# Two edits to the attention half of a fused block: a rewritten order around a pair's values, and half of the band bars as a minimum on VectorE

## What is computed

```
S  = einsum('bcqd,bckd->bcqk', Qc, Kwin)          # 64 queries against 128 keys of two windows
As = [S[band]]                                     # only 64 of the 128 keys count: key > query, key <= query + 64
for l in 1..4: As.append(q . pooled keys of the window before)     # 8 pooled keys a level
mn = min over levels of max(A)
exps = [exp(A - mn) for A in As]
esum = exps[0].sum() + sum(scale_l * exps[l].sum())
out = (exps[0] @ Vwin + sum(scale_l * exps[l] @ Vpooled_l)) / esum
```

## Time and profile before

| | |
|---|---|
| time, median of 3 runs | 287.54 us (284.66 to 290.64) |
| the profiled execution's own time | 287.94 us |
| its span in the profile | 286.1 us |
| mean granted clock of TensorE | 0.964 |
| TensorE matmul busy | 268.0 us, 94% |
| VectorE busy | 161.8 us, 57% |
| ScalarE busy | 149.5 us, 52% |
| GpSimd busy | 134.7 us, 47% |

### The profile page before, as it was taken

How to read it: one execution, slowest core, us unless ns; L and a number is a source line. 1 busy time by engine, 2 the same in 40 slices (tenths; PEclk the granted TensorE clock), 3 DMA queues, 4 the chain that set the end, 5 groups by cost and what they waited for, 6 DMA issues and landing times.

```text
span 286.1 us, 7311 instructions
## 1 busy us (share of the span) xinstructions
PE 268.0 (94%) x2713; PEld 222.8 (78%) x2713; DVE 161.8 (57%) x463; ACT 149.5 (52%) x308; POOL 134.7 (47%) x231
## 2 busy tenths in 40 slices
PE   7999996989997999689989999999999999999994
PEld 6768774878886898659979896778888678888883
DVE  7782460643345402422792266878786987777763
ACT  6764633543474452713738356544686555555551
POOL 7751300230122146204161304886884778888881
PEclk9998898697999999959999999999999999999999
DMA  7211157304009666369675110000000000000000
GB/s 221 61 56 62 57 113 242 73 13 129 2 19 336 231 173 184 94 161 290 135 176 142 39 23 21 2 10 10 11 10 9 10 11 10 9 11 19 9 10 21
DMA packets 19107, 23.04 MB, mean 81 GB/s; under 512 B 8248, under 2 KB 14136, under 8 KB 19072
## 3 DMA queue, kind: packets, MB, share of 16 engines
q1 hardware_dynamic: 17952, 21.69, 26.9%
q10 hardware_dynamic: 1120, 0.89, 1.1%
HBM read 10.93 MB, written 5.24 MB: 57 GB/s over the span
## 4 chain that ended last, share of the span: by engine, by line
PE 69%; DVE 10%; DMA 9%; issue 4%; ACT 3%; SPq 2%; POOL 0%; ACTq 0%; DVEq 0%
PE bank L1138 11%; PE bank L1140 10%; PE bank L1139 10%; PE bank L1330 8%; PE bank L1306 4%; PE bank L1309 4%; DMA k_rows<-arena 3%; PE bank L1292 3%; PE bank L1219 2%; PE bank L1274 2%; PE bank L1181 2%; PE bank L1334 2%; DMA xres<-x 2%; DVE work L1121 2%; PE bank L1232 2%
## 5 line engine op out<-in xcount | busy, mean ns | idle before, releaser
L744 POOL TENSOR_TENSOR work<-work 128x256 f32<-128x256 f32 x110 | 81.7, 747 | 31.5 <-DVE work L1121 18.9
L1121 DVE SCALAR_TENSOR_TENSOR work<-bank,comb,work 128x256 f32<-128x256 f32 x128 | 59.0, 481 | 25.4 <-ACT work L885 23.7
L885 ACT ACTIVATE work<-bank 128x256 f32<-128x256 f32 x128 | 48.5, 385 | 45.6 <-PE bank L1140 41.9
L860 ACT ACTIVATE work<-bank 128x512 f32<-128x512 f32 x64 | 34.8, 594 | 44.1 <-PE bank L1309 32.9
L1330 PE MATMUL bank<-work,vaug 128*64 128x64 f32 x1024 | 42.3, 231 | 0.0
L1330 PEld LDWEIGHTS bank<-work,vaug 128*64 128x64 f32 x1024 | 36.9, 143 | 4.4 <-ACT work L860 0.4
L650 POOL COPY vaug<-vwin 128x64 f32<-128x64 f32 x64 | 12.2, 236 | 53.1 <-PE bank L1334 53.0
L1306 PE MATMUL bank<-bar,ident_r 128*128 128x512 f32 x64 | 31.9, 499 | 1.1 <-issue 0.9
L1309 PEld LDWEIGHTS bank<-qmk,kst 98*128 98x128 f32 x128 | 26.0, 203 | 5.0 <-issue 1.8
L1309 PE MATMUL bank<-qmk,kst 98*128 98x256 f32 x128 | 26.8, 292 | 0.0
L1139 PE MATMUL bank<-arena,xT_hi 128*128 128x512 f32 x64 | 25.1, 392 | 0.0
(11 more groups left out here) (220 smaller groups left out, 541.9 us busy)
## 6 DMA issues: line engine op xcount, KB each, us to landing
w_stage<-w SPq DMA_DIRECT2D x8, 512.0 KB, 4.4
qmk<-qst SPq DMA_DIRECT2D x20, 96.0 KB
qst<-arena SPq DMA_DIRECT2D x12, 128.0 KB, 3.9
kst<-arena SPq DMA_DIRECT2D x9, 128.0 KB, 3.2
qst<-q_rows SPq DMA_DIRECT2D x3, 384.0 KB, 3.9
qmk<-q_rows SPq DMA_DIRECT2D x12, 96.0 KB
p_rows<-kpool SPq DMA_DIRECT2D x2, 512.0 KB, 3.8
attT<-denom SPq DMA_DIRECT2D x8, 128.0 KB, 2.6
```

What stands on the lines that cost most here:

```text
L744: gp.tensor_tensor(gacc[t % 2][:, :], gacc[t % 2][:, :], gtmp[(adds - 1) % TMP_RING][:, :], ALU.add).then_inc(acc_done, 1)
L860: act.activation(prob[lo % P_RING][:, :, :, :], bank[sc % SCORE_BANKS][:, :].rearrange("p (c j q) -> p c j q", c=2, j=GH), ACT.Exp).then_i ...
L885: act.activation(sig[hn % SIG_RING][:, :], bank[hn % HID_BANKS][:, HID:2 * HID], ACT.Sigmoid).then_inc(sig_done, 1)
L1121: dve.scalar_tensor_tensor(dst[:, :], bank[hn % HID_BANKS][:, 0:HID], comb[:, t, e:e + 1], sig[hn % SIG_RING][:, :], ALU.mult, ALU.mult).t ...
```

## The change

Two edits. BARRED_BY_PE shrinks from all eight tiles of a unit to (0, 1, 4, 5): the tiles k = 2, 3, 6, 7 lose the matmul of L1306 and get the minimum of L1060 on VectorE. In the order, ("norm", u) and ("values", u, h) no longer wait in a list for the next out with k % 4 == 1: norm follows directly behind the outs of its step and values at the end of that step. Guards and shift of the next unit, and its transposition and load one step later, stand ahead of the `beside` work of their step and no longer within it. For u = 1 and u = 3 the guards begin at score 4 instead of 3 and 2. ("pl", 1) and ("kp", 1) move from the end of unit 1 and the start of unit 2 to steps 2 and 4 of unit 2.

```
-GUARD_AT = [4, 3, 2, 2, 2, 2, 2]
+GUARD_AT = [4, 4, 2, 4, 2, 2, 2]
...
         s.append(("out", u, k))
-        if k % 4 == 1:
-            s.extend(norms)
-            norms.clear()
         if k % 4 == 3:
             norms.append(("values", u, k // 4))
...
-            7: [("apply", 1, 1)], 8: [("xT", 1, 0)], 9: [("pl", 1)]},
-        2: {0: [("xT", 1, 1)], 1: [("kp", 1)], 3: [("qk", 1, 0, 0)], 4: [("qk", 1, 0, 1)], 5: [("kd", 4)], 6: [("qk", 1, 1, 0)],
+            7: [("apply", 1, 1)], 8: [("xT", 1, 0)]},
+        2: {0: [("xT", 1, 1)], 2: [("pl", 1)], 3: [("qk", 1, 0, 0)], 4: [("qk", 1, 0, 1), ("kp", 1)], 5: [("kd", 4)], 6: [("qk", 1, 1, 0)],
...
             while len(local) > LAG:
                 attend()
+            s.extend(n for n in norms if n[0] == "norm")
+            if u + 1 < UNITS and i == GUARD_AT[u] + 2:
+                s += [("shiftT", u + 1), ("shift load", u + 1)]
+            if u + 1 < UNITS and i == GUARD_AT[u]:
+                s += [("guard", u + 1, 0), ("guard", u + 1, 1), ("shift", u + 1)]
             for n in (i, i + 1):
                 s += beside.get(u, {}).get(n, [])
-                if u + 1 < UNITS:
-                    first = GUARD_AT[u]
-                    if first <= n < first + 2:
-                        s.append(("guard", u + 1, n - first))
-                    if n == first + 1:
-                        s.append(("shift", u + 1))
-                    if n == first + 2:
-                        s.append(("shiftT", u + 1))
-                    if n == first + 3:
-                        s.append(("shift load", u + 1))
+            s.extend(n for n in norms if n[0] == "values")
+            norms.clear()
...
-BARRED_BY_PE = tuple(range(NB // 2))
+BARRED_BY_PE = (0, 1, 4, 5)
```

## The result

| | before | after |
|---|---|---|
| median of 20 runs each, us | 288.27 (284.66 to 293.38) | 280.85 (274.48 to 288.92) |
| ratio, 95% interval | | 0.961 [0.956, 0.967] |
| profiled execution: time, span | 287.94, 286.1 | 277.70, 275.9 |
| mean granted clock of TensorE | 0.964 | 0.975 |

The kernel became 7.4 us faster by the medians (279 was forecast from a before of 288), and 10.2 us by the two profiled executions. Medians here are over all runs; the ratios leave disturbed runs out. All lines of after stand six lower than in the kernel before: the bar L1306 is L1300, the minimum L1060 is L1054, the first score tiles L1292 are L1286, an out's matmuls L1330 are L1324, guards L1219 are L1213.

A forecast was written before the change was run, and what follows sets the result against it. TensorE sets the attention's pace, through matmuls, few long waits and stretches at 1.2 GHz. Stretch gains sum to 14.3 us; less 3.4 for one slow stretch and 2 for unfollowed VectorE waits leaves 8.9, so 279 us, range 271 to 287.

The forecast's parts named there:

- Up to the first score of unit 1: Start to 46.24 us: shift transposed ahead of kp, its load issued earlier; gain 3.0 us, 0.9 of it bars, bounds 2 to 3.5.
- To the pair 4, 5 of unit 1: Up to 54.86 us: the slow 6.83 us takes half at 2.4 GHz if the wait nearly goes; gain 3.4 us, else 0.
- To the first score of unit 2: 54.86 to 66.40 us: VectorE's work delays out 3 and the shift load; 10.6 us for 11.54, gain 0.9.
- To the guards of unit 5, and to the spread: Units 2 and 3 to 109.13 us: gain 1.8 us; unit 4 to 121.53, norm earlier: gain 2.6, bounds 1 to 3.6.
- To the guards of unit 6: Up to 129.8 us: unit 5's keys and queries 4 us sooner, slow stretch gone; gain 3.4 us, else 0.
- Units 5 to 7: Bars -2.8 us against VectorE's queue in unit 6 +2.5, ScalarE +0.5, last minima +0.6: loss 0.8, against 0 to +4.
- Bars that go: 32 matmuls of L1306 at 0.23 us each come off TensorE: 7.4 us, 0.93 a unit, counted inside the stretches.
- TensorE slower at large: Rival: fewer dense matmuls and short waits lower the clock in all units, 3.4 us a unit; 292 to 299 us; chance 0.07.
- VectorE in the way: Rival: minima delay the shift or an out in most units, none of the slow stretches gone; 286 us; chance 0.27.
- All slow stretches go: Rival: every stretch at 1.2 GHz goes, the 68.04 one too; gain 16 us, so 272; chance 0.20.
- The edit doesn't act: Rival: weight loads the bars cover come to light, a third of 0.23 us lost each, 2.5 us; inside the forecast.
- Minima that come: 32 minima on VectorE at 0.71 us each, 22.7 us in all, hidden as a sum; about 1.9 each beside GpSimd.

The follow-up runs named there:

- e1: The kernel before with only half of the bars (tiles 2, 3, 6, 7 on minima), old order kept: 293.8 us, ratio 1.014.
- e13: e2 with guards, shift, transposition and load put back inside the beside work, with the old guard starts: 279.2 us, ratio 0.974.
- e2: The changed kernel with all bars on TensorE as before and no minimum, so the new order alone: 279.3 us, ratio 0.968.
- e8: The changed kernel with unit 1's second statistics and the normalisation behind them moved to score 6, behind the shift's load: 279.1 us, ratio 0.970.
- e10: e2 with norm put back behind the next out with k % 4 == 1: 285.0 us, ratio 0.992.
- e9: e8 plus two SyncE moves: unit 2's output gather ahead of w1's loads, unit 5's keys and head queries ahead of unit 3's gather: 274.8 us, ratio 0.954.
- e4: The changed kernel with neither bars nor minima for tiles 2, 3, 6 and 7: 281.1 us, ratio 0.975.
- e11: e2 with the same three moves as e9, all bars on TensorE and no minimum: 275.9 us, ratio 0.956.
- e3: The changed kernel with its 32 minima and all 64 bars issued on TensorE as well: 281.0 us, ratio 0.970.
- e5: The changed kernel with no bar at all and 64 minima on VectorE: 289.0 us, ratio 0.998.
- e14: e5 with all 64 bars issued on TensorE besides: 287.7 us, ratio 0.989.

## Why the prediction was right in the time and wrong in some of its reasons

**Up to the first score of unit 1.** Right in the mechanism: 3.8 us in the profiled execution (46.24 to 42.44) for 3.0. Some of it is chance: the prediction counted three stretches at 1.2 GHz in the attention, and the fourth, at 27.08 to 30.50, lies in front of this score. e1 and e13, which keep the old place of the load and don't have that stretch, start it at 40.98 and 41.11, wait 2.7 us or more, and reach the score at 44.99 and 45.23. So the move is worth 2.6 to 2.8 us. The 0.9 for bars in the 3.0 was nothing: e2, with all of them, reaches it at 42.41.

**To the pair 4, 5 of unit 1.** Half right: the slow stretch shrank from 6.8 to 3.4 us, gain 2.0 for 3.4. The reserve in the sum, that one of two slow stretches stays, was in the right size: 3.4 us of each stayed.

**To the first score of unit 2.** Right in place and price: 10.69 for the 10.6 forecast, with VectorE's operations ahead of the load, and a wait of 1.1 before an out and 1.1 before unit 2. e8 shows that these two waits hang on the statistics and the normalisation.

**To the guards of unit 5, and to the spread.** 1.9 for 1.8, then 1.65 for 2.6. The second was short because norm was not free to run: its ScalarE copies stood ready but waited 1.75 us for the gather of unit 2 (4.43 us, issued behind SyncE's w1 loads), a queue that I had not followed. In e10, with norm back, TensorE waits 2.2 us at the spread again. In the same stretch I took two VectorE operations of the earlier trace rows for 0.65 us each when alone; L459 takes 0.48 at the median of its eight, and one of them had grown to 2.60.

**To the guards of unit 6.** Wrong by 2.5: 0.9 for 3.4. The slow stretch halved, but the pooled keys of unit 6, which queue behind those of unit 5 that I had coming 4 us sooner, came 2.3 us too late for TensorE. e9 mends that, and with the other two moves gives 6 us.

**Units 5 to 7.** 1.0 of loss for the 0.8 forecast, right by luck in part: half of the new slow stretch at 146.86, 1.7 us, is in it, which the step didn't have. No part of it was tested by itself.

**Bars that go. This is the step that failed.** I counted 32 x 0.23 = 7.4 us of it in the sum, 0.93 in each unit. The duration was right; that it comes off the time was not. By e2 and e4 half of it (3.6) reaches the rest; 2.1 us show up as more idle time in the profiled executions, and where the remainder goes isn't shown. The minima take back 2.1 (e4 to after), with idle up by another 2.5; that leaves 1.5. And 6.6 us more at 1.2 GHz in after than in e2 would take 3.0; these two means have errors of 1.8 and 1.9 us and come from different groups, and e9 and e11 don't repeat the difference, so this last part is not shown for after. What is shown is the outcome: in the new order, three pairs that differ in the second edit or its bars alone (e2 and after, e3 and after, e11 and e9) are within 1% of each other. So the second edit is worth nothing within 1%, and the first edit made the gain. That the total came out right is in part luck: the profiled execution of after had 13.7 us at 1.2 GHz where its 20 runs have 23.4 on average. The steps above sum to some 10 us, of which 6.8 us less at 1.2 GHz make 3, while the medians show 7.4.

**The rivals.** *TensorE slower at large* named the mechanism that ate this step: fewer dense matmuls, more time at 1.2 GHz. I gave it 0.07 because I had it as three to six more slow units; at half the bars it is between nothing (e11 to e9) and 5 us (e2 to e4, 11.2 us more at 1.2 GHz), and at no bars (e5, 46.8 us at 1.2 GHz) it eats everything. The Trainium skill (TensorE: Matmul & The Clock Gate, A second HAM failure mode: psum-queue depth-cycling) told of a clock that swings when short idles lie between groups of matmuls. In e5 it does swing, to 0.85 in the attention; but in e14 it came back at an idle total of 17.0 for 19.2 us, so that in this kernel the bars mattered and not the idle total alone. *VectorE in the way*: three waits of at most 1.1, and 1.3 to 2.1 us of rest by e3 and e4, a small part of it. The prediction's own sign of being wrong on the clock, an attention below 0.93, didn't show in the profiled execution of after (0.95), which is one of its fastest; an estimate from the mean of its runs is 1 - 23.4 / (2 x 140) = 0.92. *All slow stretches go* and *The edit doesn't act* were not seen.

**Minima that come.** 686 ns at the median, 749 as a mean, for 710. The Trainium skill (GPSIMD Engine Reference, 8. Key points) has GpSimd contend with instructions of two SBUF inputs; three of 32 showed it, at up to 1.88 us, and some 12 others that ran beside GpSimd didn't.

## What to carry to other kernels

Before counting work that leaves the busiest engine as time, ask what that engine will wait for next, and whether the work was the dense part that kept its clock up: here 7.4 us of matmuls were worth nothing, and moving an output copy and a load ahead of other work, which took 4.5 us off the idle time, made the whole gain. Change the order first and the share of work second, and time each alone. And in a kernel whose runs differ by some per cent, compare the time at each clock level before comparing medians: executions of one program differed here by up to 28 us at 1.2 GHz.

## What was not expected of the hardware

- The spread between runs of one program, 14 us in after, goes nearly all with the time at 1.2 GHz: 0.46 us for each microsecond of it.
- Adding 64 matmuls of 512 columns that do nothing for the result (e5 to e14) took 25 us off the time at 1.2 GHz and left the kernel no slower: 287.7 us for 289.0.
- The same matmuls in slightly different orders can settle at quite different clocks: e13 had 9.7 us at 1.2 GHz in the mean, e2 16.8, e10 26.2. This stays unexplained.
- A minimum of 128x512 in fp32 beside GpSimd is either untouched (0.69, some 12 times in after) or lengthened (3 times, by as much as 1.2 us; by up to 2.1 us in e5). The Trainium skill (VectorE: DVE Perf Modes, The TRN2 errata — SBUF-src ops pay a fixed extra latency per instruction) gives (N + 151) / 0.96 ns for an addition of two fp32 tiles, 691 for N = 512; the median of the minima here was 686.
